# A gated attention-and-FFN block on one core: unread products in TensorE's prologue, the first chunk's exponentials in PSUM, two row preparations on ScalarE, and new orders for every queue

## The reference

```python
x = x + tanh(g_xattn) * wkv(w, u, k=layernorm(x), v=ctx)
x = x + tanh(g_ffn)   * ffn(layernorm(x))
# wkv, for every sequence and channel, over the steps (stabilised in the reference):
#   y_t = (p + e^{u+k_t} v_t) / (q + e^{u+k_t});  p = e^w p + e^{k_t} v_t;  q = e^w q + e^{k_t}
# ffn: f = hadamard(x * SU_ug); h = silu(f W_gate^T * s_g) * (f W_up^T * s_u)
#      out = (hadamard(h * SU_dp) W_down^T) * Wscale_dp        (256 -> 1024 -> 256)
```

## Time and profile before

| | |
|---|---|
| median of 3 runs | 108.43 us (108.34 to 108.54) |
| the profiled execution | 109.38 us, its span 107.6 us |
| TensorE busy | 94.2 us, 88% of the span |
| VectorE, ScalarE, GpSimd busy | 71.8, 62.9, 53.2 us |
| mean granted clock of TensorE | 0.981 of 2.4 GHz |

### The profile page before, as it was taken

One profiled execution on the slowest core, in us unless ns is written; L12 is line 12 of the kernel. 1 busy time (PEld: TensorE's weight loads), 2 busy tenths in 40 slices (PEclk: granted clock), 3 DMA queues, 4 the chain that ended last, 5 costly groups with the idle time before them and its releaser, 6 DMA issues.

```text
span 107.6 us, 1995 instructions
## 1 busy us (share of the span) xinstructions
PE 94.2 (88%) x702; PEld 88.3 (82%) x702; DVE 71.8 (67%) x155; ACT 62.9 (58%) x137; POOL 53.2 (49%) x77
## 2 busy tenths in 40 slices
PE   0048918998999999999999999999999999999990
PEld 0026807775978899999999999999999999999980
DVE  0397999748989989599997998895523513321331
ACT  1394377199998266499927529966644443224410
POOL 5068936427499957450270775345554223422320
PEclk9999998599999999999999999999999999999998
DMA  2999999400000000000000020000200000020002
GB/s 52 262 333 389 418 391 400 182 0 0 9 0 0 0 3 0 9 0 0 0 0 0 6 97 0 0 0 9 93 5 0 0 6 0 0 97 0 0 0 98
DMA packets 3729, 7.69 MB, mean 71 GB/s; under 512 B 484, under 2 KB 904, under 8 KB 3720
## 3 DMA queue, kind: packets, MB, share of 16 engines
q1 hardware_dynamic: 3396, 7.34, 18.3%
q10 hardware_dynamic: 324, 0.23, 1.1%
HBM read 6.52 MB, written 1.05 MB: 70 GB/s over the span
## 4 chain that ended last, share of the span: by engine, by line
PE 82%; DVE 5%; DMA 3%; issue 2%; POOL 2%; ACT 2%; DVEq 0%; POOLq 0%
PE UG L1008 43%; PE OD L1059 13%; PE KZ L1059 8%; DMA X<-in_x 3%; PE UG L923 3%; PE FX L963 3%; PE FX L978 3%; PE UG L917 2%; DVE DEN L775 2%; DVE SQ L712 1%; PE KZ L894 1%; PE KZ L899 1%; PE UG L944 1%; PE VB L988 1%; PE VB L1000 1%
## 5 line engine op out<-in xcount | busy, mean ns | idle before, releaser
L420 POOL TENSOR_TENSOR HL<-H,HH 128x256 fp32r<-128x256 f32 x31 | 24.8, 804 | 30.4 <-ACT HH L671 30.4
L865 DVE SCALAR_TENSOR_TENSOR H<-S,ALPHA,UG 128x256 f32<-128x256 f32 x32 | 15.0, 476 | 13.4 <-ACT S L680 13.3
L680 ACT ACTIVATE S<-UG,CV 128x256 f32<-128x256 f32 x32 | 15.1, 471 | 13.7 <-PE UG L1008 13.5
L1008 PE MATMUL UG<-FH,WTH 128*128 128x256 f32 x128 | 21.8, 292 | 0.4 <-DVE FH L829 0.4
L1008 PE MATMUL UG<-FL,WTH 128*128 128x256 f32 x128 | 21.0, 286 | 0.0
L1008 PE MATMUL UG<-FH,WTL 128*128 128x256 f32 x128 | 20.5, 283 | 0.0
L1008 PEld LDWEIGHTS UG<-FH,WTH 128*128 128x128 f32 x128 | 17.7, 191 | 1.7 <-ACT WTL L625 0.7
L1008 PEld LDWEIGHTS UG<-FL,WTH 128*128 128x128 f32 x128 | 17.7, 191 | 0.5 <-issue 0.5
L1008 PEld LDWEIGHTS UG<-FH,WTL 128*128 128x128 f32 x128 | 17.6, 191 | 0.0
L671 ACT ACTIVATE HH<-H 128x256 fp32r<-128x256 f32 x32 | 13.2, 412 | 4.8 <-DVE H L865 4.7
L1059 PE MATMUL OD<-HH,MH 128*128 128x256 f32 x40 | 11.3, 283 | 0.0
(11 more groups left out here) (142 smaller groups left out, 195.2 us busy)
## 6 DMA issues: line engine op xcount, KB each, us to landing
WN<-in_weights SPq DMA_DIRECT2D x4, 512.0 KB, 9.1
DN<-in_w_down SPq DMA_DIRECT2D x2, 512.0 KB, 7.6
out<-XT SPq DMA_DIRECT2D x3, 256.0 KB, 2.5
X<-in_x SPq DMA_DIRECT2D x2, 256.0 KB, 4.0
V<-in_ct SPq DMA_DIRECT2D x2, 256.0 KB, 7.8
XT<-in_xt SPq DMA_DIRECT2D x2, 256.0 KB, 8.3
X<-in_x SPq DMA_DIRECT2D x1, 512.0 KB, 9.3
V<-in_ct SPq DMA_DIRECT2D x1, 512.0 KB, 11.6
```

The source lines that it names most:

```text
L420: eng.tensor_tensor(HL[:, q % JT, 0:n], ring(H, q), HH[:, q % JT, 0:n].bitcast(F32), ALU.subtract).then_inc(done, 1)
L680: act.activation(ring(S, q), gate_part(q), ACT.Silu, scale=VT[:, V_SGATE + j:V_SGATE + j + 1]).then_inc(silu_ready, 1)
L865: dve.scalar_tensor_tensor(out=ring(H, q), in0=ring(S, q), scalar=ALPHA[:, j:j + 1], in1=up_part(q), op0=ALU.mult, op1=ALU.mult).then_inc( ...
L1008: return pe.matmul(dst, w[:, m, j, t, :], f[:, g, t, :], start=start, stop=stop, skip_group_check=True)
```

## The change

1. TensorE gets a stage `busy`: one fp32 product of 256 columns (the Hadamard matrix with the first 256 columns of the constants) into the bank that the next filling will overwrite; nobody reads it. Six of them stand in the prologue: two ahead of `center`, one after `w` 0, one after `w` 2, two after `fwht_x`. `fwht_x` itself moves behind `w` 0 to 2, and `w_rest` 2 behind `spread`.
2. Group 0's exponentials go to PSUM: the half t = 0 to bank OD, t = 1 to the upper half of KZ. `av` of group 0 becomes two instructions. `keys` 1 waits in both engines until `mix_den` and `av` of group 0 have read that half.
3. `rows` (ScalarE, two Relu) replaces two of `setup_rows`' instructions on VectorE, and `steps` moves from GpSimd to ScalarE, behind `signs`.
4. The loads have another order, and all four queues too: some stages change their engine (`fly` 1, 2, 4, 5, 6, `w_lo` 6, one `x_lo`) and many change their slot.

```diff
 PE_STAGES = {
-    -1: [("center", 0), ("keys", 0), ("fwht_x", 0), ("w", 0), ("w", 1), ("w", 2), ("w_rest", 0), ("keys", 1), ("fwht", 0), ("w", 3),
-        ("w_rest", 1), ("ones", 0), ("w_rest", 2), ("m", 0), ("spread", 0), ("w_rest", 3)],
+    -1: [("busy", 0), ("busy", 1), ("center", 0), ("keys", 0), ("w", 0), ("busy", 2), ("w", 1), ("w", 2), ("busy", 3), ("fwht_x", 0),
+        ("busy", 4), ("busy", 5), ("w_rest", 0), ("keys", 1), ("fwht", 0), ("w", 3), ("w_rest", 1), ("ones", 0), ("m", 0), ("spread", 0),
+        ("w_rest", 2), ("w_rest", 3)],
 ACT_STAGES = {
-    -1: [("setup", 0), ("signs", 0), ("tanh", 0), ("decay", 0), ("ratio", 0), ("keys", 0), ("recip", 0), ("gated", 0), ("w_hi", 0),
-        ("w_hi", 1), ("w_hi", 2), ("keys", 1), ("square", 0), ("w_hi", 3), ("w_lo", 0), ("f_copy", 0), ("w_hi", 4), ("w_hi", 5),
-        ("w_lo", 1), ("w_lo", 2), ("w_lo", 3), ("w_hi", 6), ("norm1", 2), ("m_hi", 0), ("recip", 1), ("keys", 2)],
+    -1: [("setup", 0), ("tanh", 0), ("rows", 0), ("signs", 0), ("steps", 0), ("decay", 0), ("keys", 0), ("ratio", 0), ("gated", 0),
+        ("recip", 0), ("w_hi", 0), ("w_hi", 1), ("w_hi", 2), ("w_lo", 0), ("keys", 1), ("square", 0), ("w_hi", 3), ("w_hi", 4),
+        ("w_lo", 1), ("w_hi", 5), ("f_copy", 0), ("m_hi", 0), ("w_lo", 2), ("w_lo", 3), ("w_hi", 6), ("norm1", 2), ("recip", 1),
+        ("keys", 2)],
-    1: [("w_hi", 7)],
-    2: [("m_hi", 2), ("x_hi", 1)],
-    3: [("square", 1)],
-    4: [("m_hi", 3)],
-    5: [("f_copy", 1), ("f_hi", 1)],
+    2: [("m_hi", 2)],
+    3: [("m_hi", 3), ("x_hi", 1), ("w_hi", 7), ("square", 1), ("f_copy", 1)],
+    6: [("f_hi", 1)],
...
 DVE_STAGES = {
-    -1: [("stats1", 0), ("setup_rows", 0), ("norm1", 0), ("stats1", 1), ("center", 0), ("scan_a", 0), ("av", 0), ("mix_den", 0),
-        ("scan_av", 0), ("mix_num", 0), ("estimate", 0), ("newton", 0), ("fly", 3), ("fly", 4), ("fly", 2), ("scan_a", 1), ("var", 0),
-        ("stats1", 2), ("mix_den", 1), ("f_scaled", 0), ("f_lo", 0), ("outs", 0), ("fly", 7), ("x1", 0), ("m_lo", 0), ("av", 1),
-        ("alpha", 0), ("scan_av", 1)],
-    0: [("m_lo", 1)],
-    1: [("mix_num", 1), ("estimate", 1)],
-    2: [("newton", 1), ("x1", 1), ("m_lo", 2), ("x_lo", 1), ("stats1", 3)],
-    4: [("w_lo", 7), ("var", 1), ("m_lo", 3)],
+    -1: [("stats1", 0), ("outs", 0), ("setup_rows", 0), ("alpha", 0), ("norm1", 0), ("stats1", 1), ("center", 0), ("scan_a", 0),
+        ("av", 0), ("mix_den", 0), ("scan_av", 0), ("mix_num", 0), ("estimate", 0), ("newton", 0), ("fly", 1), ("fly", 3), ("scan_a", 1),
+        ("fly", 6), ("fly", 5), ("var", 0), ("stats1", 2), ("f_scaled", 0), ("f_lo", 0), ("mix_den", 1), ("fly", 7), ("x1", 0),
+        ("av", 1), ("m_lo", 0), ("scan_av", 1)],
+    0: [("m_lo", 1), ("mix_num", 1)],
+    1: [("estimate", 1)],
+    2: [("newton", 1), ("x1", 1), ("m_lo", 2), ("x_lo", 1), ("w_lo", 6), ("w_lo", 7), ("av", 2)],
+    3: [("stats1", 3), ("var", 1), ("m_lo", 3)],
...
 POOL_STAGES = {
-    -1: [("rstd1", 0), ("setup_shift", 0), ("steps", 0), ("rstd1", 1), ("norm1", 1), ("fly", 0), ("error", 0), ("fly", 1), ("fly", 6),
-        ("rstd2", 0), ("rstd1", 2), ("fly", 5), ("fly", 10), ("fly", 11), ("error", 1), ("w_lo", 5), ("w_lo", 4)],
-    0: [("w_lo", 6)],
+    -1: [("rstd1", 0), ("setup_shift", 0), ("rstd1", 1), ("norm1", 1), ("fly", 0), ("error", 0), ("fly", 2), ("fly", 4), ("rstd2", 0),
+        ("rstd1", 2), ("fly", 10), ("error", 1), ("fly", 11), ("w_lo", 5), ("w_lo", 4)],
...
+        def exps_half(g, t):
+            return KZ[:, GT:2 * GT].rearrange("p (b q) -> p b q", b=GB) if g == 0 and t else exps(g)[:, t, :, :]
...
             load_x(1)
-            load_ctx(0)
             load_xt(0)
-            load_down(0)
             load_w(0)
             load_w(1)
+            load_xt(1)
+            load_ctx(0)
+            load_down(0)
             load_down(1)
-            load_x(2)
             load_w(2)
             load_w(3)
             load_ctx(1)
+            load_x(2)
+            load_xt(2)
             load_ctx(2)
-            load_xt(1)
-            load_xt(2)
...
+                elif name == "steps":
+                    act.wait_ge(step_clear, 1)
+                    act.wait_ge(step_in, 16)
+                    act.activation(STEPR[0:32 + CT, :], STEP[:, :], ACT.Copy).then_inc(steps_r, 1)
+                elif name == "rows":
+                    act.wait_ge(row_in, 16)
+                    act.wait_ge(plus_clear, 1)
+                    act.activation(WPLUS[0:CT, :], VR[:, :], ACT.Relu).then_inc(w_pos, 1)
+                    act.activation(POSW[:, :], VR[:, :], ACT.Relu).then_inc(w_pos, 1)
...
+                    if g == 1:
+                        act.wait_ge(den_ready, 1)
+                        wait_shared(act, "av", 0)
...
+                elif name == "busy":
+                    item = FILLS[UNREAD[g]]
+                    wait_bank_free(pe, item)
+                    pe.wait_ge(const_in, 16)
+                    pe.matmul(fill(item)[:, 0:2 * P], HAD, CV[:, 0:2 * P], start=True, stop=True, skip_group_check=True)
```

More of the change, by code:

```diff
@@ L108 @@
+    13: [("f_scaled", 2), ("f_lo", 2), ("mix_num", 3), ("error", 3)],
+    16: [("estimate", 3), ("newton", 3)],
+    17: [("x1", 3)],
+    19: [("var", 3)],
+    20: [("f_scaled", 3), ("f_lo", 3)],
 }
 POOL_STAGES = {
[L110 to L113 removed]
@@ L114 @@
-    3: [("rstd2", 1), ("rstd1", 3)],
+    -1: [("rstd1", 0), ("setup_shift", 0), ("rstd1", 1), ("norm1", 1), ("fly", 0), ("error", 0), ("fly", 2), ("fly", 4), ("rstd2", 0),
+        ("rstd1", 2), ("fly", 10), ("error", 1), ("fly", 11), ("w_lo", 5), ("w_lo", 4)],
+    1: [("sum", 1)],
+    2: [("rstd2", 1)],
+    5: [("rstd1", 3)],
     9: [("sum", 2)],
     10: [("rstd2", 2)],
-    19: [("sum", 3)],
-    20: [("rstd2", 3)],
+    17: [("x_lo", 3), ("sum", 3)],
+    19: [("rstd2", 3)],
 }
@@ L146 @@
         FILLS += [("up", q)] if width(q) == GT else [("gate", q), ("up", q)]
-    FILLS += [item for item in PE_STAGES.get(q, []) if item[0] in ("m", "w")]
+    for item in PE_STAGES.get(q, []):
+        if item[0] in ("m", "w"):
+            FILLS.append(item)
+        elif item[0] == "busy":
+            UNREAD[item[1]] = len(FILLS)
 INDEX = {item: n for n, item in enumerate(FILLS)}
@@ L244, in build @@
             "tanh_gate", "decay_low", "decay_exp", "c_ready", "m_ready", "ratio_ready", "decay_set", "alpha", "outs"))
-        signs, wplus, steps_r, centers, at_ready = (sem(n) for n in (
-            "signs", "wplus", "steps_r", "centers", "at_ready"))
+        signs, w_pos, wplus, steps_r, centers, at_ready = (sem(n) for n in (
+            "signs", "w_pos", "wplus", "steps_r", "centers", "at_ready"))
         filled, m_full, m_hi, m_left, w_full, w_hi, w_left, ni_ready = (sem(n) for n in (
@@ L358, in states, with flat @@
             return tile[:, 0:CT * GT].rearrange("p (t b q) -> p t b q", t=CT, b=GB)
+        def flat(tile):
+            return tile.rearrange("p t b q -> p (t b q)")
         def lanes(tile):
@@ L377, in multiply_values @@
                 eng.wait_ge(den_ready, g + 1)
-            eng.tensor_tensor(lanes(values(g)), lanes(exps(g)), lanes(V[:, g, :, :, :]), ALU.mult).then_inc(done, 1)
+            if g == 0:
+                for t in range(CT):
+                    i = eng.tensor_tensor(values(g)[:, t, :, :], exps_half(g, t), V[:, g, t, :, :], ALU.mult)
+                i.then_inc(done, 1)
+            else:
+                eng.tensor_tensor(lanes(values(g)), lanes(exps(g)), lanes(V[:, g, :, :, :]), ALU.mult).then_inc(done, 1)
         def reciprocal_error(eng, g, done):
@@ L711, in scan @@
                     part = slice(t * CT * GT // n, (t + 1) * CT * GT // n)
-                    dve.tensor_tensor_scan(tile[:, part.start + 1:part.stop + 1], D0[:, :, :, :].rearrange("p t b q -> p (t b q)")[:, part],
-                                           steps[:, part], 0.0, ALU.mult, ALU.add).then_inc(done, 1)
+                    dve.tensor_tensor_scan(tile[:, part.start + 1:part.stop + 1], flat(D0[:, :, :, :])[:, part],
+                                           steps[t], 0.0, ALU.mult, ALU.add).then_inc(done, 1)
                 dve.wait_ge(done, scans(tile, g) - 1)
@@ L759, in stage @@
                         dve.wait_ge(a_ready, CT * (g + 1))
-                    scan(SQ, g, exps(g).rearrange("p t b q -> p (t b q)"), scanned_a)
+                    scan(SQ, g, [exps_half(g, t).rearrange("p b q -> p (b q)") for t in range(CT)] if g == 0 else [flat(exps(g))], scanned_a)
                 elif name == "scan_av":
@@ L766, in stage @@
                     wait_shared(dve, "av", g)
-                    scan(SP_, g, values(g).rearrange("p t b q -> p (t b q)"), scanned_v)
+                    scan(SP_, g, [flat(values(g))], scanned_v)
                 elif name == "mix_den":
```

63 lines of the change are left out of this document (24 added, 39 removed).

## The result

The changed kernel takes 107.63 us in the median of 7 runs (107.26 to 108.14), the kernel before 108.36 us beside it (7 runs, 107.93 to 108.54). The ratio is 0.9947, with a 95% interval of 0.9922 to 0.9973: 0.5% faster, where the prediction had 2.5 us or 2.3%. The profiled execution took 107.55 us, its span 105.7, so it is an ordinary one. The profiled execution of before was not. Its 109.38 us lie above all of that kernel's seven runs. The ratios leave out executions that took over 1.5% more than the fastest of their kernel, most of those in which TensorE's clock fell and a few in which it did not; these matter here, so the tables count them all.

A forecast was written before the change was run, and what follows sets the result against it. Slot 0's start, ahead of a solid block of TensorE products, bounds the kernel. Terms summed to 3.44 us, less 0.4 for holes: 109.38 - 3.0 = 106.4 us profiled, median 105.9 us, range 104.9 to 107.8.

The forecast's parts named there:

- The clock: TensorE before slot 0: unread products and shorter holes hold the granted clock, saving 1.80 us in FX and transposes.
- two readings: Median 0.95 us under profile: the profile's own cost (105.4), or ordinary runs lacking part of the dip (106.4); middle 105.9.
- the two terms: The clock's savings on TensorE's path to slot 0: 1.44 us in FX and 0.36 us in the transposes.
- ctx: VectorE's product with ctx: V lands near 11.1 us in the new load order, so `av` starts 0.37 us earlier.
- ctx comes late: Rival: ctx lands at 12.4 instead of 11.1 us, the chain gives back 1.3 us, 107.2 us; chance 0.12.
- The denominator: VectorE before y: exponentials in PSUM avoid the stall beside GpSimd's butterfly, 1.90 us becomes 0.87, 1.03 saved.
- The unread products: Six fp32 products in TensorE's prologue, 0.225 us each at full clock, placed where TensorE waits; costed at nothing.
- The early part: ScalarE's prologue: two Relu shift GG by 0.65 us, STEPR near 7.5; product with ctx could start 0.6 us earlier.
- The order behind y: Between y and slot 0: `w_rest` 2 behind `spread` takes 0.34 us off the path; `f_copy` goes behind four ScalarE steps.
- a cover without slack: ScalarE's `f_copy` ends at 21.75 us, so slot 0 can't start before 22.2; the sum gave 22.4.
- VectorE in slot 2: Rival: group 1's x stays at 36.83 us, holding H of slot 3 and slot 6; 108.8 us, chance 0.09.
- The clock didn't fall: Judges the rival that TensorE's clock falls all the same in the prologue: 1.80 us comes back, 107.3 us; chance 0.22.

The follow-up runs named there:

- e1: The kernel before, unchanged, run again: 107.76 us at full clock, ratio 1.0013.
- e2: The changed kernel without its six unread products: 107.88 us at full clock, ratio 1.0000.
- e12: The changed kernel, unchanged, run again on another occasion: 107.97 us at full clock, ratio to before 0.9989.
- e13: The changed kernel without its six unread products, a repeat for more executions: 107.72 us at full clock, ratio 1.0001.
- e7: The kernel before with only group 0's exponentials moved to the two PSUM banks: 107.64 us at full clock, ratio 0.9965.
- e5: The kernel before with only the new order of the loads: 107.74 us at full clock, ratio 0.9970.
- e6: The changed kernel with group 0's exponentials in SBUF again: 107.72 us at full clock, ratio to before 0.9980.
- e10: The changed kernel with ctx loaded early, `fwht_x` ahead of the weight tiles, four unread products between `keys` 1 and y: 107.43 us at full clock, ratio 0.9925.
- e14: The kernel before with the six unread products alone, two ahead of `center`, four behind `w` 2: 108.61 us at full clock, ratio 1.0061.
- e9: The kernel before with group 0's exponentials in PSUM and ALPHA moved behind `center`: 106.81 us at full clock, ratio 0.9890.
- e15: Repeat of the kernel before with exponentials in PSUM and ALPHA moved behind `center`: 106.69 us at full clock, ratio 0.9907.
- e4: The changed kernel with ctx loaded early and the reciprocal's correction ahead of GpSimd's first butterfly: 107.36 us at full clock, ratio to before 0.9954.
- e11: The changed kernel with ctx loaded early, `fwht_x` ahead of the weight tiles, only two unread products: 106.81 us at full clock, ratio to before 0.9939.

## Why the prediction was wrong

**The bound was right.** Slots 0 to 31 are a solid block, 79.06 us against 78.86, and everything hangs on slot 0's start.

**The clock was the step that failed.** "In sum the dip costs 1.80 us on the path" is near the 1.55 us between the two profiles of before (e1), and false as a term of the sum. The median of before has no dip. I saw that the profiled execution lay 0.95 us over the median and split the difference between two readings. The full reading was that the profile showed a rare execution: 109.38 minus the dip of 1.55 is 107.8, about the median of before in most experiments. Without the two terms the same sum is 3.44 - 1.80 - 0.4 = 1.24 us, and from the median of 108.43 it gives 107.2. What is left of the term is 0.1 us in the mean of before. So the clock had 1.3 of the 2.5 us that were forecast.

**ctx: the mechanism was right, the size was off by 1.0 us.** It landed at 12.12, not at 11.1 (and at 12.02 to 12.65 in the profiles of e2, e12 and e13). The rate of 336 KB a us was read between 6.55 and 13.40. In the new order the third slice moved only 223 GB/s, and the issue of V itself took 1.15 us on SyncE instead of 0.43. That is the rival "ctx comes late", at 12.1 instead of the 12.4 that I gave it. So `av` started 0.67 us later than in the earlier trace rows where the sum had it 0.37 earlier. Without the clock and with ctx where it landed, the sum has 0.2 us left (1.24 - 1.04); the two profiles at full clock have 0.1 (0.31 - 0.21), the medians 0.73 in the first result and -0.13 in e12.

**The denominator: size right, cause half right.** It took 0.87 us, 1.03 less. Splitting `av`, for which the sum had 0.1 us, cost nothing: the denominator starts 0.67 us behind `av`, where it was 0.71. PSUM does this alone (e7), the load order does it alone (e5), and in the changed kernel only one can count (e6). The sum had the gain of the one and the cost of the other (ctx at 11.1) in it, and missed that in the new order the butterfly is no longer there to collide with.

**The unread products cost nothing, as said, in this place** (e2, e13). But each counted 0.43 us at full clock, not 0.225: the earlier trace rows has "x4" for what the trace shows as two entries for each fp32 product, and I read a group's count as instructions. The error did no harm in the changed kernel, whose holes were long enough. In e10 the four products took twice the time that was meant for them. The Hadamard part FX, whose x8 are four fp32 products, was sized to 0.17 us all the same (1.80 against 1.97), since I compared entries with entries.

**The early part.** I had GG 0.65 us late. It came 0.1 us early, at 6.36. `tanh` and the first Relu were done before the constants landed, and these landed at 4.7 us, 0.5 earlier than in the first profile of before, so that GG waited only for the second Relu, until 5.10. The two Relu took 0.4 us each, 0.3 apart:

```profile
4.49 0.40 ACT L577 ACTIVATE WPLUS<-VR 2x256 fp32r<-2x256 f32 x1
4.79 0.40 ACT L578 ACTIVATE POSW<-VR 2x256 f32<-2x256 f32 x1
5.10 1.26 ACT L601 ACTIVATE GG<-CV 128x128 fp32r<-128x128 f32 x4
...
7.16 0.31 ACT L572 ACTIVATE STEPR<-STEP 34x128 fp32r<-34x128 f32 x1 [0.60 <-DMA STEP<-in_steps]
```

STEPR waited 0.60 us for its own transfer, and was ready at 7.47 as predicted. None of this counts, since ctx binds.

**The order behind y.** `w_rest` 2 off the path: right, 0.34. The Hadamard product of the down weights and the sums took 0.16 and 0.13 us more than in the profiled execution of before, which the sum did not have. The copy of FX, called a cover without slack, was done at 22.5 and was not waited for. The sum for slot 0 from the two measured profiles is 0.40 (y) + 1.27 + 0.41 (clock) + 0.34 - 0.29 = 2.13, against 2.10 read.

**The other rivals.** VectorE in slot 2: x of group 1 was done at 34.80 and no hole came of it, as the cover had it. The clock didn't fall in 19 executions. With the products where the change puts them it fell in 0 of 31 (the first result, e6, e12), and in 0 of 12 in e14. Without any it fell in 12 of 188 (before, e2, e13, e5, e7, e9, e15). At that rate 43 executions would escape by chance in 6 of 100 cases. That pool mixes kernels; the changed kernel alone, 4 of 24 without the products and 0 of 31 with them, would come out so by chance in 3 of 100. So it is likely, not shown, that the products hold the clock here. e4 (5 of 12) and e10 (1 of 12) show that they don't in every schedule. Nor does the length of a hole alone decide, as the prediction took it: the clock held behind 1.68 us (e1) and 2.08 us (e14), and fell in e11 behind holes of 1.04 and 1.10.

**ALPHA was in no step.** The change moves it to the start of the prologue, where it takes 0.17 us. In the kernel before it stands ahead of the second scan of group 1, and the profiles show what it can cost there: from slot 0 to the end of the span it is 81.7 to 81.8 us without the stall (e1, e9, e15), and 82.3 to 82.7 with it (e5, e14, e7). How often it stood in the way in ordinary executions of before is not known, since only few were profiled. So how much of the measured 0.5% is ALPHA's is open.

## What to carry to other kernels

Compare the profiled execution with the median before you cost anything from it: if it is 1% longer and holds a dip of the clock, run it again, because the dip may be in one execution of twenty. A stall between two engines has several cures, another place for the operand, another time for the other engine, and they don't add up. After a reordering, look for small operations with two SBUF inputs beside GpSimd's long ones: moving an 8-column operation gave 0.6 to 1.0 us on top of e7, at least as much as the whole change.

## What the runs showed of the hardware

A VectorE operation of 8 columns with both inputs in SBUF took 1.27 to 1.29 us when it was issued just as a GpSimd step began (e5, e7, e14), and 0.16 us when it came between two steps (before, e1). In all five profiles it started 1.69 to 1.70 us behind the first of the two steps, so hundredths of a us decide. The denominator took 1.88 us beside such a step from SBUF and 0.86 us with one input in PSUM (e1, e7). The Trainium skill (SBUF — State Buffer, "Who interferes with whom") says that a VectorE instruction with two SBUF inputs contends with a GpSimd instruction that reads SBUF, and that issue order decides who blocks. The runs agree, and show that an instruction of 8 columns is held for the whole step just as one of 256 is.

The kernel before had its full-clock executions spread from 106.9 to 109.0 us, one of 190 aside. The version of e9, in which both of these meetings are gone, kept within 106.6 to 107.2. That a tie between two engines makes the spread fits this, but no run isolates it. The landing of x (4.24 to 4.68 us in three profiles), which the start of slot 0 follows, and the slow start of TensorE differ between executions too.

The fastest version whose clock held in every execution is e9, two small edits of the kernel before: 106.81 and 106.69 us, ratios 0.9890 (0.9847 to 0.9932) and 0.9907 (0.9874 to 0.9939), against the changed kernel's 107.63 and 107.97.
